# A four-block transformer step on one core: first integers moved into attention, weight products moved ahead of routing, dispatch awaited tile by tile

## What is computed

```python
x = x + gat(ctx_512, layernorm(x))      # two graph-attention layers, 8 heads, 256 x 256 scores each
x = x + moe(layernorm(x))               # 16 experts of 176, top 4, capacity 128, and a shared expert of 352
x = x + latent_attention(layernorm(x), ctx_512)   # 16 heads; scores through products of the weights
x = x + quantised_ffn(layernorm(x))     # 704 hidden

# latent attention: q_hk = h Wq^T; q_big = q_hk w_kc_q; q_r = q_big W_qr; k_r = kv_rope W_kr
# scores = q_r k_r^T; out = ((softmax(scores) kv_rope) w_kc_kv^T) Wo^T
# quantised_ffn, per row:
#   s = 127 / max(max|x|, 1e-5); xq = clip(round(x s), -128, 127) / s
#   x1, x3 = split(xq w13^T); g = relu(x1)^2 * x3; inner = rmsnorm(g) * norm_w
#   out = quantise(inner) w2^T
```

## Time and profile before

| | |
|---|---|
| median of 3 runs | 555.82 us (555.39 to 558.62) |
| profiled execution | 556.21 us, span 554.4 us |
| mean granted TensorE clock | 0.957 of 2.4 GHz |
| busy | PE 477.1 (86%), PEld 317.1, DVE 354.7 (64%), ACT 270.9 (49%), POOL 152.7 us (28%) |
| chain of waits by engine | PE 61%, DVE 20%, ACT 6%, issue 6%, POOL 5% |
| stages, by their first work | graph attention to 162, routing to 185, dispatch to 213, experts to 248, gathers to 303, latent attention to 492, feed-forward to the end |

### The profile page before, as it was taken

One profiled execution on the slowest core, in us unless ns is written; L12 is line 12 of the kernel. 1 busy time (PEld: TensorE's weight loads), 2 busy tenths in 40 slices (PEclk: granted clock), 3 DMA queues, 4 the chain that ended last, 5 costly groups with the idle time before them and its releaser, 6 DMA issues.

```text
span 554.4 us, 9661 instructions
## 1 busy us (share of the span) xinstructions
PE 477.1 (86%) x3268; PEld 317.1 (57%) x3268; DVE 354.7 (64%) x1103; ACT 270.9 (49%) x678; POOL 152.7 (28%) x225
## 2 busy tenths in 40 slices
PE   3797899998686999998986899899999956798896
PEld 2464566665454545773564576676676734475553
DVE  4798999999748931233773755656555487357662
ACT  2486788886453313332124465465356244145661
POOL 0000000001150006705478344234333243022340
PEclk9998999998997999999997899999999999699996
DMA  8990000000150405972238000000000000000000
GB/s 212 328 201 6 1 2 1 4 1 2 29 130 1 175 10 152 285 208 86 59 93 88 9 1 2 1 1 1 1 2 2 0 1 1 1 1 9 21 19 30
DMA packets 28370, 30.15 MB, mean 54 GB/s; under 512 B 4673, under 2 KB 26402, under 8 KB 28066
## 3 DMA queue, kind: packets, MB, share of 16 engines
q1 hardware_dynamic: 25554, 24.74, 15.8%
q0 software_dynamic: 1536, 4.20, 4.4%
q10 hardware_dynamic: 1232, 0.60, 0.4%
HBM read 26.38 MB, written 3.15 MB: 53 GB/s over the span
## 4 chain that ended last, share of the span: by engine, by line
PE 61%; DVE 20%; ACT 6%; issue 6%; POOL 5%; DMA 1%; ACTq 0%; DVEq 0%
PE bank L872 5%; PE bank L768 5%; PE bank L862 5%; PE bank L850 4%; PE bank L823 4%; POOL arena L1852 4%; PE bank L782 3%; PE bank L584 3%; PE bank L935 3%; PE bank L838 3%; DVE work L1396 3%; PE bank L595 3%; PE bank L968 3%; ACT work L1203 3%; PE bank L604 2%
## 5 line engine op out<-in xcount | busy, mean ns | idle before, releaser
L1203 ACT ACTIVATE work<-bank,nmx 128x256 f32<-128x256 f32 x128 | 58.8, 472 | 61.2 <-DVE nmx L1647 61.1
L1863 POOL TENSOR_SCALAR work<-work,R 128x256 f32<-128x256 f32 x128 | 61.4, 495 | 65.8 <-DVE R L1659 65.8
L1396 DVE CUSTOM_DVE_ANT_0 work<-bank,Nw 128x256 f32<-128x256 f32 x128 | 46.5, 420 | 9.2 <-PE bank L570 9.1
L862 PE MATMUL bank<-halves,kvb 128*64 128x256 f32 x256 | 38.0, 418 | 15.3 <-DVE halves L1638 15.3
L1647 DVE TENSOR_REDUCE nmx<-bank 128x2 f32<-128x512 f32 x64 | 41.2, 684 | 12.0 <-PE bank L850 11.7
L850 PE MATMUL bank<-work 64*128 64x256 f32 x256 | 44.2, 419 | 3.2 <-ACT work L1203 3.0
L1852 POOL DMA_INDIRECT arena<-eout,idx x32 | 31.7, 991 | 30.8 <-DMA eout<-work 21.5
L1056 ACT ACTIVATE bank<-bank 128x512 f32<-128x512 f32 x64 | 34.9, 595 | 9.5 <-PE bank L570 9.5
L838 PE MATMUL bank<-ident,work 128*128 128x128 f32 x256 | 36.1, 287 | 4.0 <-POOL work L1863 4.0
L1796 POOL TENSOR_TENSOR rstd<-veps,half 128x2 f32<-128x2 f32 x12 | 8.9, 742 | 102.5 <-DVE veps L1325 102.5
L1063 ACT ACTIVATE work<-bank 128x512 f32<-128x512 f32 x64 | 35.0, 601 | 3.4 <-PE bank L584 3.4
(11 more groups left out here) (218 smaller groups left out, 929.4 us busy)
## 6 DMA issues: line engine op xcount, KB each, us to landing
work<-in_wg SPq DMA_DIRECT2D x16, 176.0 KB, 3.6
work<-in_wu SPq DMA_DIRECT2D x16, 176.0 KB, 4.3
work<-in_wd SPq DMA_DIRECT2D x16, 176.0 KB
arena<-in_wq SPq DMA_DIRECT2D x1, 2048.0 KB, 9.8
arena<-in_woT SPq DMA_DIRECT2D x1, 2048.0 KB, 16.4
eout<-work SPq DMA_DIRECT2D x16, 128.0 KB, 3.4
arena<-in_kcqT SPq DMA_DIRECT2D x1, 1536.0 KB, 21.6
arena<-in_w13T SPq DMA_DIRECT2D x1, 1408.0 KB, 8.2
```

The lines of the kernel that those rows point to most:

```text
L862: mm = pe.matmul(bank[4 + j % 2][h * CD:(h + 1) * CD, 0:S], kvb[:, m, :], ET2[:, j % 2, h, m, :], start=m == 0, stop=m == 1, tile_position ...
L1203: act.activation(E2[:, j % 2, t, h, :], bank[h][:, t * S:(t + 1) * S], ACT.Exp, bias=nmx[:, j % 2, h, t:t + 1], accum_out=S2[:, j % 2, h, ...
L1396: dve.tensor_tensor_reduce(L[:, i % 4, t, :], bank[XB[i % 4]][:, t * S:(t + 1) * S], maskN[:, g, t, :], 1.0, -3.4e38, ALU.add, ALU.max, M[ ...
L1863: pool.tensor_scalar(E2[:, j % 2, t, h, :], E2[:, j % 2, t, h, :], R2[:, j % 2, h, t:t + 1], 1.0, ALU.mult, ALU.mult).then_inc(en2_ready, 1)
```

## The change

1. *Fold of the weights.* New functions `factor_transposes` and `third_products` hold the code of lines 732 and 738. The eight transposes and the third products of groups 0 and 1 are now done in step `PAIRS + 7` of the graph attention's tail, ahead of the last `ln_transposes`; the products of groups 2 and 3 stand after the transposes of the logits, ahead of the wait for `sel_ready`. ScalarE's copies move with them: two dK and two nT copies into step `PAIRS + 7`, the other two nT copies stay behind the routing exponential.
2. *`lgT`* moves out of `smid`, which dK now overlaps at that time, to the place of `disp`.
3. *Dispatch* waits for one mask at a time in the first half k of each group.
4. *First integers.* Statistics of batches 0 and 1 and integers of tiles 0 to 3 move to attention batch 2: statistics after the reciprocals of j = 4 and 7, integers after those of j = 5, 6 and of the next batch's j = 0, 1. They write to a new buffer `centred` instead of `xln`. Statistics of batch 2 stay at j = 2 of the last batch, integers of tiles 4 and 5 come at j = 8 and 9, those of tiles 6 and 7 in turns 2 and 4 of the loop. GpSimd's roots, TensorE's transposes and ScalarE's copies follow.
5. *Turn 5 of the loop.* ScalarE's `ff_back_evac(6)` stands after `ff_integers(6)`, ahead of `ff_square(7)`; it was the first work of turn 6.

```diff
+        lgT = work[0:E, place[0]:place[0] + T]
...
+            def factor_transposes():
+                for q in range(2):
+                    pe.wait_ge(dT_evac, q + 1)
+                    for j in range(4 * q, 4 * q + 4):
+                        mm = pe.transpose(bank[2 + q][:, j % 4 * P:(j % 4 + 1) * P], dT[:, j, :], ident[:, :])
+                    mm.then_inc(d_mm, 1)
+
+            def third_products(qs):
+                for q in qs:
+                    pe.wait_ge(dT_evac, 2)
+                    pe.wait_ge(d_evac, 2 if q >= 2 else 1)
+                    for h in range(4 * q, 4 * q + 4):
+                        mm = pe.matmul(bank[q][h % 2 * CD:(h % 2 + 1) * CD, h % 4 // 2 * D:(h % 4 // 2 + 1) * D],
+                                       dK[:, h // 2, h % 2 * CD:(h % 2 + 1) * CD], wq[:, h, :], start=True, stop=True,
+                                       tile_position=(0, h % 2 * CD))
+                    mm.then_inc(nT_mm, 1)
...
+                if s == PAIRS + 7:
+                    factor_transposes()
+                    third_products((0, 1))
...
+            third_products((2, 3))
             pe.wait_ge(sel_ready, 1)
...
             for g in range(4):
-                pe.wait_ge(disp_ready, (g + 1) * NT)
                 for k in range(KT):
                     pe.wait_ge(disp_evac, max(n - 1, 0))
                     for t in range(NT):
+                        if k == 0:
+                            pe.wait_ge(disp_ready, g * NT + t + 1)
...
-                pe.wait_ge(f_q1T, min(n + 5, NT))
+                pe.wait_ge(f_q1T, (4, 5, 6, 7, 7, 8, 8, 8)[n])
...
-                if j >= 5:
+                if 5 <= j <= 8:
                     ff_in_transposes(j - 5, 0)
...
-                if n + 5 < NT:
-                    ff_in_transposes(n + 5, n + 1)
+                if n in (0, 1, 2, 4):
+                    ff_in_transposes((4, 5, 6, None, 7)[n], n + 1)
...
             for n in range(-2, NT):
-                if n >= 0:
+                if 0 <= n and n != NT - 2:
                     ff_back_evac(n)
                 if n + 2 < NT:
                     ff_relu(n + 2)
                 if 0 <= n + 1 < NT:
                     ff_integers(n + 1)
+                if n == NT - 3:
+                    ff_back_evac(n + 1)
                 if n + 2 < NT:
                     ff_square(n + 2)
...
+                    if b == B - 2 and j in (4, 7):
+                        i = (j - 4) // 3
+                        layernorm_stats(i, base, f_veps, keep_at=i)
+                    if b == B - 2 and j in (5, 6):
+                        ff_first(j - 5, base)
                 for j in range(2):
...
+                    if b == B - 2:
+                        ff_first(j + 2, base)
...
-                if j in (2, 3, 4):
-                    layernorm_stats(j - 2, base, f_veps, keep_at=j - 2)
+                if j == 2:
+                    layernorm_stats(2, base, f_veps, keep_at=2)
                 if j < AH // 2:
                     att_inverse(B - 1, j)
-                if 3 <= j <= 8:
-                    ff_first(j - 3, base)
+                if j >= AH // 2:
+                    ff_first(j - 4, base)
...
-                if n in (0, 1):
-                    ff_first(6 + n, base)
+                if n in (2, 4):
+                    ff_first(5 + n // 2, base)
```

More of the change, by code:

```diff
@@ L171, in build @@
         smid = at([3, 512])
-        lgT = smid[0:E, 0:2, :].rearrange("p a c -> p (a c)")
         IH = IE // 2
@@ L727, in _ @@
             mm.then_inc(rank_mm, 1)
-            for q in range(2):
-                pe.wait_ge(dT_evac, q + 1)
-                for j in range(4 * q, 4 * q + 4):
-                    mm = pe.transpose(bank[2 + q][:, j % 4 * P:(j % 4 + 1) * P], dT[:, j, :], ident[:, :])
-                mm.then_inc(d_mm, 1)
-            for q in range(4):
-                pe.wait_ge(dT_evac, 2)
-                pe.wait_ge(d_evac, 2 if q >= 2 else 1)
-                for h in range(4 * q, 4 * q + 4):
-                    mm = pe.matmul(bank[q][h % 2 * CD:(h % 2 + 1) * CD, h % 4 // 2 * D:(h % 4 // 2 + 1) * D],
-                                   dK[:, h // 2, h % 2 * CD:(h % 2 + 1) * CD], wq[:, h, :], start=True, stop=True,
-                                   tile_position=(0, h % 2 * CD))
-                mm.then_inc(nT_mm, 1)
             for q in range(4):
@@ L1127, in _ @@
                                        ACT.Copy).then_inc(dT_evac, 1)
+                    for q in range(2):
+                        act.wait_ge(d_mm, q + 1)
+                        act.activation(dK[:, 4 * q:4 * q + 4, :].rearrange("p j c -> p (j c)"), bank[2 + q][:, :],
+                                       ACT.Copy).then_inc(d_evac, 1)
+                    for q in range(2):
+                        act.wait_ge(nT_mm, q + 1)
+                        act.activation(nT[:, 2 * q:2 * q + 2, :].rearrange("p j d -> p (j d)"), bank[q][:, :],
+                                       ACT.Copy).then_inc(nT_evac, 1)
             for c in range(2):
@@ L1133, in _ @@
             act.activation(prob[:, :, :], prob[:, :, :], ACT.Exp).then_inc(route_exp, 1)
-            for q in range(2):
-                act.wait_ge(d_mm, q + 1)
-                act.activation(dK[:, 4 * q:4 * q + 4, :].rearrange("p j c -> p (j c)"), bank[2 + q][:, :],
-                               ACT.Copy).then_inc(d_evac, 1)
-            for q in range(4):
+            for q in range(2, 4):
                 act.wait_ge(nT_mm, q + 1)
@@ L1288, in _ @@
                     ff_integers(n + 1)
+                if n == NT - 3:
+                    ff_back_evac(n + 1)
                 if n + 2 < NT:
                     ff_square(n + 2)
-                if n >= 0 and n + 5 < NT:
-                    ff_in_evac(n + 5)
+                if n in (0, 1, 2, 4):
+                    ff_in_evac((4, 5, 6, None, 7)[n])
         @block.vector
@@ L1674, in ff_first @@
                 dve.wait_ge(f_rstd, b + 1)
-                link(dve.tensor_scalar(xln[:, t, :], row(b, t), fstat[:, b, 2 * t:2 * t + 1], fstat[:, b, 4 + t:5 + t],
+                link(dve.tensor_scalar(centred[:, :], row(b, t), fstat[:, b, 2 * t:2 * t + 1], fstat[:, b, 4 + t:5 + t],
                                        ALU.subtract, ALU.mult), base)
-                link(dve.tensor_reduce(amax1[:, n:n + 1], xln[:, t, :], AX_X, ALU.max,
+                link(dve.tensor_reduce(amax1[:, n:n + 1], centred[:, :], AX_X, ALU.max,
                                        apply_absolute_value=True), base)
@@ L1871, in _ @@
                 for j in range(2, AH // 2):
+                    if b == B - 2 and j == 5:
+                        ff_root(0)
                     normalise(b, j)
+                if b == B - 2:
+                    ff_root(1)
                 for j in range(2):
                     normalise(b + 1, j)
-            def ff_root(b):
-                root(b + 1, f_veps, f_rstd, fveps[:, b, :], fstat[:, b, 4:6])
             for j in range(2, AH // 2):
-                if j in (2, 3, 4):
-                    ff_root(j - 2)
+                if j == 3:
+                    ff_root(2)
                 normalise(B - 1, j)
```

7 lines of the change are left out of this document (5 added, 2 removed).

## The result

The changed kernel takes 554.05 us (median of 12 runs, 551.54 to 556.91) against 557.53 for the kernel before on the same chips. The ratio is 0.9956, 95% interval 0.9938 to 0.9974: a gain of 2.5 us, or 3.5 by the medians, where 9.8 was forecast. The profiled execution took 555.58 us with a span of 553.8, where before it was 556.21 and 554.4. I use both.

The account below looks back on a forecast made before the run. Bounds: a serial chain in routing, TensorE in batch 2's query steps, VectorE in the last batch and loop. Terms -1.6+4.8-15.4+2.4 = -9.8 take 556.2 to 546.4, less 0.4 for the median: 546.0 us, range 541 to 551.

Parts of the forecast that it names:

- Routing, -1.6: Routing up to dispatch: logits 3.1 us later, 5.7 gone after the rank sums, 1.0 back through low clock.
- the clock's +1.0: Routing: low clock after TensorE's idle time would now fall on the output-weight products, costing 1.0 us.
- Batch 2, +4.8: Attention batch 2: integers and statistics moved into its steps would make it 4.8 us slower, ends 0 and +6.5.
- the third set falls in the last step: +2.3: End of batch 2: third set of integers, in a step of period 3.67 us, delays the output by 2.3.
- Last batch, -15.4: Last attention batch, freed of integers: 9.9 us less between maxima and 5.5 less in the tail.
- maxima term, -9.9: Last batch: four distances between VectorE's maxima shrink from 24.54 us to 14.6 without integers.
- Loop, +2.4: Feed-forward loop: last gate 1.8 us later through tile 7's late integers, back copy 0.6 more; ends 0 and +4.8.
- rival (c): Loop: clock falls while TensorE waits for tile 7, product costs up to 2.4 us more, total 548.4; chance 0.22.
- (a): Batch 2 takes the integers for nothing, VectorE being half busy: 4.8 us less, total 541.2; chance 0.13.
- (b): The feed-forward loop hides its integers: 0 there, total 543.6; chance 0.12.
- (d): Another wait paces the last batch at 4.88 us a step, not 3.65: 4.9 more, total 550.9; chance 0.07.
- (e): Last batch runs at 1.2 GHz, losing 9.4 us of gain and the tail's 2: total 557.4; chance 0.03.

Follow-up runs that it names:

- after: First profiled execution of the changed kernel: 555.58 us, span 553.8.
- change_again: The changed kernel unaltered, run again on another chip: 553.07 us against 557.24 for the kernel before, ratio 0.994; profile span 550.5.
- third_later: Changed kernel, with batch 2's third set of integers moved beside the fourth, behind the copy its output waits for: 546.83 us, ratio 0.980 to the kernel before.
- fill_batch2: Changed kernel plus 9 unread f32 matmuls in batch 2's last step, ahead of the waiting context: 551.28 us, ratio 0.990 to the kernel before.
- under_outputs: Changed kernel, with integers of tiles 0, 1 under batch 1's output and 2, 3 under batch 2's: 546.19 us, ratio 0.982 to the kernel before.
- routing_only: Changed kernel with parts 4 and 5 undone, leaving parts 1 to 3: 553.14 us against 557.46 for the kernel before, ratio 0.993.
- routing_again: Same kernel as `routing_only`, run on another chip: 555.58 us, ratio 0.998 to the kernel before.
- before: Profiled execution of the kernel without the change: 556.21 us, span 554.4.
- combined: `under_outputs` with tiles 4, 5 after the last context copy, 6, 7 in turns 0, 1, old back copy place, fillers in routing and loop: 536.74 us, ratio 0.964.
- fill_routing: Changed kernel plus 15 unread f32 matmuls on TensorE while VectorE selects: 555.66 us, ratio 0.998 to the kernel before.
- clock_held: Changed kernel plus unread matmuls: 7 ahead of rank sums, 5 ahead of batch 2's context, 8 and 14 around tile 7: 546.07 us against 557.24, ratio 0.981.

## Why the prediction was wrong

Its direction and its steps of instructions held. What failed is the price of a wait: for the clock the sum had +1.0 in routing and nothing in batch 2, in the last batch and in the loop. Measured, the falls cost 1.2 to 2.5, 2.5 to 2.8, 1.6 and 1.7.

- **Routing, -1.6.** Counted from the second products, logits came 3.3 late for 3.1. From logits to the output-weight products it was 10.5 by the chain of waits, as from logits to factor transposes before, as planned. The failed term is the clock's +1.0: of nine profiles with these products behind the selection and no filler, two had them at 6.1 to 6.3 us and seven at 5.0 to 5.1, against 3.8 to 3.9 at full clock. From the second products to dispatch, the two profiles of the change are +0.1 and -1.1 against before, and those of the routing half -1.0 and -1.1. A further 1.4 us between dispatch and the first output in `after` (0.4 in `change_again`), in work that the change left alone, stays open. Waiting mask by mask cost nothing: dispatch runs 27.82 us for 27.81. What waiting by group would have cost in the new order no run shows.
- **Batch 2, +4.8.** With the clock taken out, it is 4.95: 5.84 less the 0.89 by which the slow context is longer. The 1.1 for each set in a query step and 2.50 for a set (2.51) are right. The exclusive port of the Trainium skill (SBUF: State Buffer, "two separate sides"), by which a set would have cost 4.0, doesn't show here: GpSimd's four normalisations (1.94 us in all, from 414.50) ran beside the set, and it took 2.51, only 0.30 more than the 2.21 of a set alone. The section binds the rule to VectorE instructions in a two-port mode or with two inputs in SBUF; which of these seven are such the runs don't show. The failed step is "the third set falls in the last step: +2.3, and the output waits behind it": I priced the stall and not what TensorE does after it. It waited 2.28 us and lost 2.8 more in `after` (2.5 in `change_again`), which is the largest single miss of the sum.
- **Last batch, -15.4.** The maxima term, -9.9, measured -10.0. The tail, planned at 12.8, was 14.66 (466.67 to 481.33). The text said that 1.5 to 2 would stay if the tail kept its low clock, and the sum didn't hold it. In `third_later`, with the tail at full clock, it is 13.0, so the steps were mis-sized by 0.2 and the fall took 1.6.
- **Loop, +2.4.** Gates after the output's start, forecast: 17.0, 23.1, 31.5, 37.8, 46.2; measured 17.0, 23.1, 31.5, 37.6, 45.9. The copy came at 48.2 (48.4). Then rival (c) happened: the product took 4.13, the last gate came at 55.4, not 54.0. The back copy cost 0.3 to 0.4, not 0.6. Rival (c) had 0.22; of seven profiles with this place of tile 7 and no filler near it, five fell whole (4.12 to 4.13), one in part (3.64, `fill_batch2`), one not at all.
- **Rivals.** (a) and (b) are out: batch 2 paid for every set in its steps, the loop for both of its own. (d) is out: maxima 3.61 to 3.71 apart. (e) is out: 14.6 us at 1.00, with PE busy 14.46 of them by the row. That is 3.6 a step and not the 2.99 of the forecast: the matmuls of the scores took 1.43 to 1.68 us in these steps for 1.13 elsewhere. Why they did is open; of the five maxima shown one waited for them, 0.18 us. The Trainium skill's rule on transposes (TensorE: Matmul & The Clock Gate, "PE-mode transpose") would join the two waits of rival (c) and make the clock fall; of the seven profiles above six agree with it and `under_outputs` does not.

The common fault is one step of reasoning. Two rows, a wait of 2.34 with no fall and one of 2.64 with a fall, were read as a line between waits that are safe and waits that aren't. The same wait in `routing_only` and `routing_again`, where nothing of that batch was changed, shows that there is no such line; this is the latter:

```profile
448.44 1.98 PE L872 MATMUL bank<-halves,kvb 128*64 128x256 f32 x8 [2.34 <-DVE halves L1652]
...
455.64 1.98 PE L872 MATMUL bank<-halves,kvb 128*64 128x256 f32 x8 [2.41 <-DVE halves L1652]
```

It is 2.34 us, to the hundredth that of before, and the clock fell. Of the 5.9 us between the forecast and `change_again` (-9.8 and -3.9 by span), 2.7 are batch 2's, 1.7 the last batch's, 1.0 the loop's, all three behind such falls, and 0.4 lie ahead of the first output. In `after` (-0.6 by span) the last three stages miss by 2.9, 1.7 and 1.2, and 3.4 lie ahead of the first output: 1.7 of it from the second products to dispatch, 1.4 between dispatch and the first output, 0.3 ahead of the second products.

## What to carry to other kernels

Price a new wait of TensorE of some 2 us with what stands behind it at half the clock, as a likely case and not as a rival, and put the wait, if it must be, ahead of short work and not ahead of the longest run of matmuls in the stage. Ask of each place on another engine not whether that engine is half idle, but which instruction stands behind it in the queue: here 2.5 us behind the reciprocal cost 1.1 or 2.3, behind the last copy ahead of 7 us of matmuls nearly nothing. Where the wait can't go, a few unread matmuls that end when it ends give the clock back; count them from a measured row, since too many can cost more than they bring: fifteen held the rank sums back by 3.0 us where seven held them back by nothing.

## What the runs showed of the hardware

- The fall of TensorE's clock after a wait is not a matter of the wait's length alone. The same instruction after the same wait fell in one run and not in another: 2.34 us (1.09 in `before`, 1.98 in `routing_again`), 2.23 us (1.61 in `after`, 1.09 in `third_later`), 2.91 and 2.92 us (4.11 in `before`, 2.23 in `routing_again`), and 1.16 us (1.91 in `combined`, 1.04 in `under_outputs`). Over all fourteen profiles TensorE waited 2.2 to 2.5 us for `halves` ahead of eight context matmuls 24 times, and 17 times they took longer than the 1.09 of full clock. After the wait of 1.16 it was one time of fourteen. The fall can also come later: in `fill_routing` the context behind the third set still took 1.09 after 2.28 us, and the output behind it 8.57. What decides between a fall and none these runs don't show. The Trainium skill (TensorE: Matmul & The Clock Gate, Part 1) says that the chip's watch on activity runs by itself and does not start with the kernel, so that one kernel's count of slow matmuls varies from run to run; the rows agree with that, and no run here tests it.
- Unread f32 matmuls of 128 x 128 by 256 columns took 0.45 to 0.48 us each (6.74 for 15, 3.29 for 7, 2.42 for 5), bf16 ones 0.12 (2.58 for 22), and both kept the granted clock at 1.00 (170 to 182 us in `fill_routing`, 519 to 526.5 in `clock_held`).
- Two chips gave 0.993 and 0.998 for one kernel, each with an interval of half a per cent that leaves the other out.
